# Combining a mixture of experts in four groups of tiles, those that the second attention reads first, and the shared weights' splits behind y

## The reference

```
x = x + ln(linear_attention(ln(x)))      # 16 heads of 128, blocks of 32, gate and output projection
x = x + ln(moe(ln(x)))
x = x + ln(window_attention(ln(x)))      # windows of 32, step 16
x = x + ln(swiglu(ln(x)))                # 1024 inner

def moe(x):                              # 2048 tokens
    scores = softmax(x @ gate_w.T)       # 16 experts, the best 2 of each token
    y = sum over the 2 of score * (silu(x @ gate_e) * (x @ up_e)) @ down_e      # inner 176
    return y + (silu(x @ shared_gate) * (x @ shared_up)) @ shared_down          # inner 352
```

## Time and profile before

| | |
|---|---|
| median of 3 runs | 1290.07 us (1285.87 to 1291.22) |
| profiled execution | 1289.32 us, its span 1287.5 us |
| TensorE busy | 1154.5 us, 90% |
| VectorE busy | 787.4 us, 61% |
| ScalarE busy | 509.2 us, 40% |
| GpSimd busy | 272.6 us, 21% |

### The profile page before, as it was taken

How to read it: one execution, slowest core, us unless ns; L and a number is a source line. 1 busy time by engine, 2 the same in 40 slices (tenths; PEclk the granted TensorE clock), 3 DMA queues, 4 the chain that set the end, 5 groups by cost and what they waited for, 6 DMA issues and landing times. The chain is left out here.

```text
span 1287.5 us, 19736 instructions
## 1 busy us (share of the span) xinstructions
PE 1154.5 (90%) x6960; PEld 1001.3 (78%) x6960; DVE 787.4 (61%) x1631; ACT 509.2 (40%) x941; POOL 272.6 (21%) x369
## 2 busy tenths in 40 slices
PE   6999999999999999999999768699975389789896
PEld 5989898988888899999898646477754377578785
DVE  4756666575657575756557759244448568675554
ACT  5674444343443433443435451122213335333322
POOL 1111101010101010101011100333248324114311
PEclk9999999999999999999999878699987569899999
DMA  4001000000000010000000070433332141000000
GB/s 139 10 1 42 1 26 16 0 33 8 0 33 8 0 41 0 33 8 0 1 1 1 12 268 1 148 107 107 99 109 69 57 116 46 21 1 2 17 17 33
DMA packets 30827, 52.43 MB, mean 41 GB/s; under 512 B 5712, under 2 KB 20016, under 8 KB 29488
## 3 DMA queue, kind: packets, MB, share of 16 engines
q1 hardware_dynamic: 26672, 40.91, 9.6%
q0 software_dynamic: 4096, 10.75, 3.3%
HBM read 36.70 MB, written 10.49 MB: 37 GB/s over the span
## 5 line engine op out<-in xcount | busy, mean ns | idle before, releaser
L619 POOL TENSOR_TENSOR linear_out_squares<-linear_out_squares,lin_sq 128x512 f32<-128x512 f32 x64 | 91.2, 1426 | 598.5 <-ACT lin_sq L520 595.5
L41 PE MATMUL lin_bank<-keep_xT_hi,lin_w_hi 128*128 128x512 f32 x384 | 155.4, 405 | 2.6 <-DVE keep_xT_lo L230 2.6
L42 PE MATMUL lin_bank<-keep_xT_lo,lin_w_hi 128*128 128x512 f32 x384 | 152.6, 397 | 0.0
L43 PE MATMUL lin_bank<-keep_xT_hi,lin_w_lo 128*128 128x512 f32 x384 | 152.3, 397 | 0.0
L575 DVE TENSOR_TENSOR lin_st<-lin_bank,lin_mask 128x512 f32<-128x512 f32 x64 | 44.3, 692 | 174.8 <-PE lin_bank L430 174.8
L516 ACT ACTIVATE lin_o<-lin_bank 128x512 f32<-128x512 f32 x64 | 38.3, 599 | 189.8 <-PE lin_bank L461 189.8
L457 PE MATMUL lin_bank<-lin_st,lin_v 128*128 128x128 f32 x512 | 94.0, 275 | 0.0
L461 PE MATMUL lin_bank<-lin_qd,lin_state 128*128 128x128 f32 x448 | 87.2, 276 | 0.0
L41 PEld LDWEIGHTS lin_bank<-keep_xT_hi,lin_w_hi 128*128 128x128 f32 x384 | 72.9, 190 | 17.9 <-issue 3.0
L43 PEld LDWEIGHTS lin_bank<-keep_xT_hi,lin_w_lo 128*128 128x128 f32 x384 | 72.5, 189 | 17.8
L42 PEld LDWEIGHTS lin_bank<-keep_xT_lo,lin_w_hi 128*128 128x128 f32 x384 | 72.7, 189 | 14.7
(11 more groups left out here) (364 smaller groups left out, 2871.1 us busy)
## 6 DMA issues: line engine op xcount, KB each, us to landing
lin_raw<-in_wp SPq DMA_DIRECT2D x8, 1024.0 KB, 4.9
sorted_y<-linear_out_acc SPq DMA_DIRECT2D x48, 128.0 KB, 2.2
experts_up_expert_up<-in_wgu SPq DMA_DIRECT2D x16, 352.0 KB, 7.5
experts_down<-in_wdn SPq DMA_DIRECT2D x16, 176.0 KB
keep_x<-in_x SPq DMA_DIRECT2D x4, 512.0 KB, 7.6
lin_raw_out<-in_wop SPq DMA_DIRECT2D x8, 256.0 KB, 2.6
tokens_x<-linear_out_acc SPq DMA_DIRECT2D x4, 512.0 KB, 9.5
linear_out_acc<-in_ffn_up SPq DMA_DIRECT2D x2, 1024.0 KB, 5.8
```

What stands on the lines that cost most here:

```text
L41: nc.tensor.matmul(out, lh, rh, start=first, stop=False, skip_group_check=skip)
L42: nc.tensor.matmul(out, lh, rl, start=False, stop=False, skip_group_check=skip)
L43: return nc.tensor.matmul(out, ll, rh, start=False, stop=last, skip_group_check=skip)
L619: pool.tensor_tensor(part, part, sq[:, a, :], ALU.add).then_inc(squares_sb, 1)
```

## The change

Three edits. First, in closing and routing, ScalarE takes the high halves of group 0 and y of the last group before it splits the shared weights; VectorE has the low halves of the shared weights' first two parts behind the low halves of group 3, the third behind the score's maximum. The array `score` moves from the weights' buffer to `keep.squares`, since it is written before the weights are split.

Second, combining has no rounds. `GroupNorm` holds one group of tiles with its own arrays and semaphores. Groups a and b are tiles 0 to 4 and 8 to 12, which hold the 528 tokens that the window attention reads of each batch row; they are weighed, normalized, added to x on VectorE, normalized again on ScalarE, and turned: four tiles whole, of the fifth 16 rows (the tail). Groups c0 and c1 are tiles 5 to 7 and 13 to 15; they are weighed, normalized on ScalarE and added to x by GpSimd, and are not turned. VectorE weighs every tile with both weights, each product linked to the one before. The gathers are issued in this order of groups. The window weights' high halves are taken behind the first step of the shared network, and their low halves on VectorE.

Third, the semaphores of the gathers and two other sets belong to the whole kernel's scope and not to their block's. Of `combine_and_norm` the new lines and what they stand among are shown.

```diff
@@ -1125,7 +1125,8 @@
         self.g_hi, self.g_lo = c.sb("g_hi", [P, KT, P], F32R), c.sb("g_lo", [P, KT, P], F32R)
         self.logits_T = c.sb("logits_T", [NE, TPS, P])
         full = lambda n, dt=F32: c.sb(n, [P, TT, NE], dt)
-        self.score, self.key, self.rest, self.one1, self.one2 = (placed(TT, NE) for _ in range(5))
+        self.score = keep.squares[:, 0:TT * NE].rearrange("p (t e) -> p t e", e=NE)
+        self.key, self.rest, self.one1, self.one2 = (placed(TT, NE) for _ in range(4))
         self.top, self.total, self.best, self.where = (c.sb(n, [P, TT]) for n in ("top", "total", "best", "where"))
         self.chosen = full("chosen", BF16)
         self.before, self.every = c.sb("before", [P, P], BF16), c.sb("every", [P, P], BF16)
@@ -1380,15 +1381,16 @@
                 dve.memset(router.gate[:], 0.0).then_inc(router.zeroed, 1)
                 output.dve_factor(dve, L, bank[0:2])
                 router.dve_gate(dve)
-                for j in range(J):
-                    net.dve_low(dve, j)
                 norms.dve_low(dve, 0)
                 norms.dve_round(dve, chain, L, lambda half: dve.wait_ge(output.y_ready, 2 * L + half + 1), split=False)
                 norms.dve_low(dve, 1)
                 norms.dve_round(dve, chain, L + 1, split=False)
                 norms.dve_low(dve, 2)
                 norms.dve_low(dve, 3)
+                net.dve_low(dve, 0)
+                net.dve_low(dve, 1)
                 router.dve_shift(dve, chain)
+                net.dve_low(dve, 2)
...
@@ -1410,10 +1412,10 @@
             def _(act):
                 output.act_root(act, L)
                 router.act_gate(act)
+                norms.act_high(act, 0)
+                output.act_take(act, L, bank[0:2])
                 for j in range(J):
                     net.act_high(act, j)
-                norms.act_high(act, 0)
-                output.act_take(act, L, bank[0:2])
                 norms.act_root(act, L, split=False)
                 router.act_logits(act, 0)
                 norms.act_high(act, 1)
...
+class GroupNorm:
+    def __init__(self, c, tag, keep, y, tiles, turned):
+        self.keep, self.y, self.tiles, self.n, self.at = keep, y, tiles, len(tiles), slice(tiles[0], tiles[0] + len(tiles))
...
+    def source(self, k):
+        return self.y if k == "y" else self.keep.x
+    def dve_stats(self, dve, chain, k, i):
+        chain.step(dve.bn_stats(self.stats[k][:, i, :], self.source(k)[:, self.tiles[i], :]))
+    def dve_spread(self, dve, chain, k):
+        chain.wait()
+        for i in range(self.n):
+            chain.step(dve.bn_aggr(self.mean_var[k][:, i, :], self.stats[k][:, i, :]))
+        chain.wait()
+        dve.tensor_scalar(self.spread[k][:], self.mean_var[k][:, :, 1], LN_EPS, None, ALU.add).then_inc(self.spread_ready[k], 1)
...
+    def dve_scale(self, dve, chain, k):
+        dve.wait_ge(self.root_ready[k], 1)
+        chain.link(dve.reciprocal(self.scale[k][:], self.root[k][:]))
+        dve.scalar_tensor_tensor(self.shift[k][:], self.mean_var[k][:, :, 0], -1.0, self.scale[k][:], ALU.mult, ALU.mult).then_inc(self.affine_ready[k], 1)
+    def act_apply(self, act, k):
+        act.wait_ge(self.affine_ready[k], 1)
+        for i, t in enumerate(self.tiles):
+            last = act.activation(self.z[k][:, i, :], self.source(k)[:, t, :], ACT.Identity,
+                                  scale=self.scale[k][:, i:i + 1], bias=self.shift[k][:, i:i + 1])
+        last.then_inc(self.z_ready[k], 1)
+    def add(self, eng):
+        eng.wait_ge(self.z_ready["y"], 1)
+        xs = self.keep.x[:, self.at, :]
+        eng.tensor_tensor(xs, xs, self.z["y"][:], ALU.add).then_inc(self.added, 1)
+    def dve_x(self, dve, chain):
+        self.add(dve)
+        dve.wait_ge(self.added, 1)
+        for i in range(self.n):
+            self.dve_stats(dve, chain, "x", i)
+        self.dve_spread(dve, chain, "x")
+    def columns(self):
+        first = self.tiles[0] * P
+        return slice(first, first + SEG), slice(first + SEG, first + SEG + TAIL_ROWS)
+    def pe_turn(self, pe, banks):
+        pe.wait_ge(self.z_ready["x"], 1)
+        for k in range(KT):
+            for j in range(TPS):
+                last = pe.transpose(banks[k][:, j * P:(j + 1) * P], self.z["x"][:, j, k * P:(k + 1) * P], self.keep.ident[:])
+            last.then_inc(self.turned, 1)
+    def pe_turn_tail(self, pe, banks):
+        pe.wait_ge(self.low, KT)
+        for k in range(KT):
+            last = pe.transpose(banks[0][:, k * TAIL_ROWS:(k + 1) * TAIL_ROWS], self.z["x"][0:TAIL_ROWS, TPS, k * P:(k + 1) * P],
+                                self.keep.ident[0:TAIL_ROWS, 0:TAIL_ROWS])
+        last.then_inc(self.turned, 1)
...
+    def dve_low(self, dve, banks):
+        at, _ = self.columns()
+        for k in range(KT):
+            dve.wait_ge(self.high, k + 1)
+            dve.tensor_tensor(self.keep.xT_lo[:, k, at], banks[k][:], self.keep.xT_hi[:, k, at].bitcast(F32), ALU.subtract).then_inc(self.low, 1)
...
 def combine_and_norm(nc, keep, sorted_y, y, window, w):
     with Scope(nc, "combine") as c:
         got = [c.sb(f"got{b}", [P, TT, HID]) for b in range(2)]
         bank = c.banks(8)
         net = Swiglu(nc, c, keep, y, bank, SHARED, SHARED_EARLY, keep.shared)
+        turn = bank[6:8]
+        own = c.sem("own")
+        used = [GroupNorm(c, f"used{b}", keep, y, list(range(b * PER_BATCH, b * PER_BATCH + USED_TILES)), True) for b in range(BATCH)]
+        rest = [GroupNorm(c, f"rest{b}", keep, y, list(range(b * PER_BATCH + USED_TILES, (b + 1) * PER_BATCH)), False) for b in range(BATCH)]
+        ORDER = [t for group in used + rest for t in group.tiles]
         STEPS = [(g, j) for g in range(SHARED_EARLY, SEGS) for j in range(net.J)]
+        arrived = keep.arrived
         with nc.Block() as block:
             @block.sync
             def _(sp):
@@ -1623,63 +1734,90 @@
             @block.gpsimd
             def _(pool):
                 window.pool_zero(pool)
+                for t in ORDER:
                     for b, slot in enumerate((keep.slot1, keep.slot2)):
                         pool.indirect_dma_start(out=got[b][:, t, :], out_offset=None, in_=sorted_y,
                                                 in_offset=bass.IndirectOffsetOnAxis(ap=slot[:, t:t + 1], axis=0)).then_inc(arrived[t], DMA)
+                for group in rest:
+                    group.add(pool)
             @block.vector
             def _(dve):
                 chain = Chain(dve, own)
+                def weigh(group, *places):
+                    for i in places:
+                        t = group.tiles[i]
+                        if t // TPS >= SHARED_EARLY:
+                            dve.wait_ge(net.y_sb, 2 * (t // TPS - SHARED_EARLY + 1))
+                        dve.wait_ge(arrived[t], 2 * DMA)
                         for b, weight in enumerate((keep.weight1, keep.weight2)):
+                            chain.link(dve.scalar_tensor_tensor(y[:, t, :], got[b][:, t, :], weight[:, t:t + 1], y[:, t, :], ALU.mult, ALU.add))
+                        group.dve_stats(dve, chain, "y", i)
+                (a, b), (c0, c1) = used, rest
+                net.dve_step(dve, chain, *STEPS[0])
+                window.dve_low(dve)
+                weigh(a, 0)
+                net.dve_step(dve, chain, *STEPS[1])
+                weigh(a, 1, 2)
+                net.dve_step(dve, chain, *STEPS[2])
+                weigh(a, 3)
+                net.dve_step(dve, chain, *STEPS[3])
+                weigh(a, 4)
+                a.dve_spread(dve, chain, "y")
+                net.dve_step(dve, chain, *STEPS[4])
+                a.dve_scale(dve, chain, "y")
+                weigh(b, 0)
+                a.dve_x(dve, chain)
+                net.dve_step(dve, chain, *STEPS[5])
+                a.dve_scale(dve, chain, "x")
+                weigh(b, 1, 2, 3)
+                a.dve_low(dve, turn)
+                weigh(b, 4)
+                b.dve_spread(dve, chain, "y")
+                a.dve_low_tail(dve, turn)
+                b.dve_scale(dve, chain, "y")
+                weigh(c0, 0)
+                b.dve_x(dve, chain)
+                weigh(c0, 1)
+                b.dve_scale(dve, chain, "x")
+                weigh(c0, 2)
+                c0.dve_spread(dve, chain, "y")
+                b.dve_low(dve, turn)
+                c0.dve_scale(dve, chain, "y")
+                b.dve_low_tail(dve, turn)
+                weigh(c1, 0, 1, 2)
+                c1.dve_spread(dve, chain, "y")
+                c1.dve_scale(dve, chain, "y")
             @block.scalar
             def _(act):
+                (a, b), (c0, c1) = used, rest
+                net.act_step(act, *STEPS[0])
+                window.act_high(act)
+                for step in STEPS[1:4]:
+                    net.act_step(act, *step)
+                a.act_root(act, "y")
+                net.act_step(act, *STEPS[4])
+                a.act_apply(act, "y")
```

(50 more changed lines are left out.)

70 lines of the change are left out of this document (29 added, 41 removed).

## The result

| | before | after |
|---|---|---|
| median, 4 runs each | 1290.64 us (1285.87 to 1294.5) | 1277.92 us (1276.58 to 1280.32) |
| ratio | | 0.9905, interval 0.9885 to 0.9924 |
| profiled execution, span | 1289.32, 1287.5 us | 1278.36, 1276.6 us |

Faster by 0.95%; 1279.4 was forecast, within 1273.5 to 1286.5.

What follows compares the result with a forecast made beforehand. The prediction took waits between engines, in serial chains through VectorE, as the bound, not TensorE. Routing's 5.9 plus combining's 4.8 gave 10.7 us off 1289.32: 1278.6, or 1279.4 on the median's scale, range 1273.5 to 1286.5.

Steps and rivals of the forecast that it cites:

- Part 1: Routing: moving the shared weights' splits gains 5.9 us; VectorE's idleness covers their return, else 2.2 us are given back.
- Part 2: Combining: the new order ends at 1018.8 against 1023.87, 5.1 us earlier, counted as 4.8.
- (a): Combining, VectorE: waits for the window weights, landing at 952.5; their low halves end at 954.3.
- (b): Combining, VectorE: three shared-network steps 5.4 us, five tiles 6.8, spread 0.7, ending at 967.2.
- (c): Combining: root, table load, silu, step, scale, apply, output, ending at 975.3; VectorE idles 6 of these 8 us.
- (d): Combining: tile 1.36 us, add 1.5, x statistics 1.7, spread, step, scale, three tiles 4.1, ending at 986.9.
- (e): Combining: low halves with waits 2.0 us, tile 1.36, spread 0.7, root, tail and scale 1.1, ending at 992.1.
- (f): Combining: second apply, add, statistics, spread, tile, scale, apply, first bank's transposes, high half, low halves, ending at 1006.3.
- (g): Combining's close through GpSimd's last add (1.8 us): 1017.4, or 1018.8 with 1.4 for GpSimd's hold on VectorE.
- rival 2: Combining: window loads land late, ScalarE and VectorE stand behind them; end up to 9.1 us later, 1288.5; chance 0.05.
- Rival 1: Combining gains nothing, handoffs longer than costed by 0.2 us at some 24 places: 1284.2; chance 0.10.
- Rival 4: Combining: GpSimd's gather issues hold VectorE's two-input operations, fully held 26.6 us, so slower, 1306; chance 0.05.

Runs made afterwards that it cites:

- route_only: Kernel before with the change's routing edits alone (order of the splits, score in other memory): 1282.58 us, ratio 0.9946.
- combine_only: Changed kernel with the routing edits undone: 1286.18 us, ratio 0.998.
- last_add_2: Changed kernel with the addition of tiles 13 to 15 moved from GpSimd to VectorE, on the third chip: 1274.96 us, ratio 0.9899 to the kernel before.
- filled: Changed kernel with last addition on VectorE, output copy first, residual-only tiles filling VectorE's waits; second chip: ratio 0.9865 to the kernel before.
- gpsimd_last: Kernel before with a 16-column memset on GpSimd behind VectorE's last low half of combining: 1290.33 us, ratio 1.0019.
- filled_2: Same kernel as filled, run on the third chip: 1265.33 us, ratio 0.982 to the kernel before.
- gpsimd_last_routing: Changed kernel with one 128x1024 memset on GpSimd behind routing's last matmuls, second chip: ratio 0.9984 to the kernel before.
- routing_late: Changed kernel with two 128x1024 memsets on GpSimd behind routing's last matmuls, third chip: 1281.64 us, ratio 0.9955 to the kernel before.

## Why the prediction was right, and where it was not

**What bounds.** Right: VectorE's chain of rounds set the end of both blocks, and the changed kernel's lead passed through the experts unchanged (6.27 at the maximum, 6.36 behind them), route_only's lost 0.5.

**Part 1.** The root was forecast at 746.2 and came at 746.24; alone the part gave 5.7 us between the medians. The lead grew by 0.40 more on the way to the maximum; what gave it was not tested. The cover for the splits' return held: 1.10 us of idleness are left ahead of the maximum and 1.89 (2.76 before) ahead of the first product's h at 766.03.

**Part 2, step by step**, in us from combining's first matmul (the forecast's moments less 944.69):

| step | forecast | trace |
|---|---|---|
| (a) window weights' low halves | 9.6 | 9.1 |
| (b) first group's spread | 22.5 | 22.0 |
| (c) tile 8 starts | 30.6 | 30.0 |
| (d) tile 11 closed | 42.2 | 41.7 |
| (e) second group's scale | 47.4 | 46.4 |
| (f) last whole low halves | 61.6 | 60.7 |
| (g) GpSimd's last addition | 74.1 | 73.2 |

The loads came at 7.43 against 7.8, so rival 2 fell. The linked product was taken at 0.51 and two take 1.00. GpSimd's hold was 1.46 against 1.4. The idle stretch ahead of tile 8 was 3.59, against "some 4". The drain that the forecast weighed and left out isn't there: 960.59 + 1.28 = 961.87, and the silu starts at 961.89. Rival 1 (handoffs eat the gain) fell by the same table: every step came earlier than forecast. Rival 4 (gathers hold VectorE) fell: beside their issues two products took 0.99 to 1.02. The work of the block became 6.0 us shorter, against 5.1, since each step was costed a little too long. Forecast and measurement both start from the trace of before, with its 1.3 us of hold on VectorE (see combine_only); from the two other traces of the old order the gain is 4.7.

**The term that was mis-sized**: "for the new scopes' and semaphores' clearing, which no row isolates, I allow 0.3 either way". The handover cost 2.65 us more than before. The forecast itself named GpSimd's addition as the block's last operation and cited no row in which GpSimd ends a block; the change of the last engine wanted a term with two ends of its own, not an allowance for clearing. With 2.65 for it the same sum gives 1281.7, also within the range. The range's low end doesn't follow from its terms: 0.6, 1.4 and 3 us below 1279.4 is 1274.4, not 1273.5; nothing hangs on it.

**What made up for it.** The 0.46 of part 1, the 0.9 of part 2, and a piece of luck: the window attention took 1.46 us less from its first matmul to its first y (74.40 against 75.86). The stretches from 32 to 40 us after its start, in the changed kernel and in before:

```profile
1046.50:1054.50 8.00, 7.25 (x54) 5.97 (x54) 6.82 (x11) 3.71 (x8) 3.15 (x3) 0.99 0.00 0
```

```profile
1056.20:1064.20 8.00, 8.00 (x45) 6.66 (x46) 5.44 (x9) 3.30 (x7) 2.56 (x2) 0.71 0.00 0
```

The granted clock is 0.99 of 2.4 GHz in the first and 0.71 in the second; the 32 us ahead of them have 0.66 in both. In stretches of 1 us one sees two levels, 1.2 and 2.4 GHz. In every trace the clock falls to the lower one 13 to 17 us into the stage, while TensorE pauses, and returns to the upper one at a moment that differs, with TensorE busy. The stage's length goes with that moment in all fourteen traces:

| clock back at 2.4 GHz, us into the stage | traces | the stage, us |
|---|---|---|
| 30 to 32 | 7, route_only among them | 73.2 to 73.8 |
| 32 to 33 | 3, the changed kernel among them | 74.3 to 74.4 |
| 36 to 37 | before, last_add_2, filled | 75.7 to 75.9 |
| 41 to 42 | gpsimd_last | 79.7 |

The code of the stage is the same in all, and the moment doesn't go with the edit: route_only, with the old combining, is in the first row, last_add_2, with the new, in the third. So the 1.46 us are luck, and a forecast should carry them as scatter.

## What to carry to other kernels

Order work by who reads it first, then use what nobody waits for as filler in the waits: the change did the first (4.7 to 6.0 us of the block's work), filled_2 did both, moved one copy as well, and its block is 10.5 us shorter than last_add_2's, with the same work. Ask of each block which engine ends it: in combining, where GpSimd had issued gathers, its last instruction cost 2.65 us at the block's end even when it was a memset of 0.11 us. A total that is met proves no term; the ledger by moments shows which failed, and a second trace of the same code shows which of its rows are luck.

## What was not expected of the hardware

- A block that GpSimd ends is followed 2.96 to 2.97 us later by the next one's first matmul, in the traces of seven kernels on all three chips, with two or three ranges of semaphores cleared; one that VectorE ends, 0.32. In routing, without gathers, GpSimd's end was followed by SyncE's first load in 0.29.
- On one chip of three the combining stage lost some 28 us while gathers were issued, with TensorE waiting for nothing that the trace shows; variants of the change had 0.9938 to 0.9984 there (filled 0.9865), so part of the change's gain may be lost on such a chip. The changed kernel itself wasn't run on it.
- Where VectorE's products of two inputs and GpSimd's addition start together, either can be the one that is held: in before VectorE's four took 3.76 us instead of 1.67, in route_only and gpsimd_last GpSimd's addition took 3.71 instead of 2.35.
- Beside a memset of GpSimd the cast of 128x48 that takes 0.19 us took 0.47 in two traces, and ended 0.05 us after the memset in both (802.69 and 802.74 in gpsimd_last_routing, 802.96 and 803.01 in routing_late), so not only operations of two inputs are held. The two operations ahead of it, beside the same memset, took their usual 0.21 and 0.20.
